# A planned transformer kernel: which matmuls the plan counts as a change, and where the next head's second projections stand

## The reference

```python
h = _attention(_rms(x, ln1_w[l]), wq[l], wk[l], wv[l], wo[l], cos, sin, causal_bias)  # 16 heads of 64, 4 key heads, causal
x = clip(res + h)
h = _moe(_rms(x, ln2_w[l]), wr[l], wg[l], wu[l], wd[l])     # router, softmax, top 2 of 8; all 8 experts computed, weighted
x = clip(res + h)
```

## Time and profile before

| | us |
|---|---|
| median of 3 runs | 3292.73 |
| profiled execution | 3282.75 |
| its span | 3280.9 |
| TensorE busy | 3071.8 (94%) |
| VectorE busy | 2605.9 (79%) |
| ScalarE busy | 2173.9 (66%) |
| GpSimd busy | 2014.9 (61%) |

### The profile page before, as it was taken

How to read it: one execution, slowest core, us unless ns; L and a number is a source line. 1 busy time by engine, 2 the same in 40 slices (tenths; PEclk the granted TensorE clock), 3 DMA queues, 4 the chain that set the end, 5 groups by cost and what they waited for, 6 DMA issues and landing times. The chain is left out here.

```text
span 3280.9 us, 50730 instructions
## 1 busy us (share of the span) xinstructions
PE 3071.8 (94%) x16864; PEld 2036.3 (62%) x16864; DVE 2605.9 (79%) x3764; ACT 2173.9 (66%) x4011; POOL 2014.9 (61%) x1573
## 2 busy tenths in 40 slices
PE   5999999799999999999999999999999999999998
PEld 3555555456666577666665776666657766666576
DVE  7788876678888678888886778888867888888677
ACT  4566667676666676766666767666667676666675
POOL 2100000377878676778776757787767677877675
PEclk8899999889999999999999999999999999999999
DMA  5442421323323065323230653233206532332053
GB/s 122 74 77 49 82 61 38 81 71 80 72 68 75 18 196 146 88 63 77 68 73 20 196 142 90 65 75 71 65 24 191 150 89 65 76 71 65 24 185 113
DMA packets 160402, 283.55 MB, mean 86 GB/s; under 512 B 32593, under 2 KB 64209, under 8 KB 159889
## 3 DMA queue, kind: packets, MB, share of 16 engines
q1 hardware_dynamic: 159632, 280.18, 33.9%
q10 hardware_dynamic: 512, 0.13, 0.0%
HBM read 88.47 MB, written 31.72 MB: 37 GB/s over the span
## 5 line engine op out<-in xcount | busy, mean ns | idle before, releaser
L1471 ACT ACTIVATE prob<-psA 128x512 f32<-128x512 f32 x1152 | 658.3, 593 | 510.7 <-PE psA L1869 328.4
L1273 POOL TENSOR_TENSOR xw<-xw,prob 128x512 f32<-128x512 f32 x672 | 872.4, 1298 | 169.3 <-ACT prob L1471 102.3
L2193 DVE TENSOR_REDUCE mxp<-psA 128x1 f32<-128x512 f32 (+3 forms) x864 | 527.6, 663 | 60.2 <-PE psA L1838 59.5
L2167 DVE RECIPROCAL rden<-psA 128x256 f32<-128x256 f32 x256 | 448.5, 1752 | 150.9 <-PE psA L1897 148.4
L1868 PE MATMUL psA<-qs,ks 128*128 128x512 f32 x1152 | 504.4, 438 | 14.3 <-ACT prob L1471 7.9
L1838 PE MATMUL psA<-ks,qs 128*128 128x512 f32 (+3 forms) x1536 | 438.4, 368 | 41.3 <-DVE ks L2295 16.8
L1273 POOL TENSOR_TENSOR xw<-prob 128x512 f32<-128x512 f32 x224 | 288.1, 1286 | 275.4 <-issue 169.9
L1869 PE MATMUL psA<-qs,ks 128*128 128x512 f32 x1152 | 454.1, 394 | 0.0
L1307 POOL TENSOR_TENSOR hidl<-gate,hidh 128x512 fp32r<-128x512 f32 x256 | 335.6, 1322 | 175.0 <-ACT hidh L1549 172.8
L1483 ACT ACTIVATE psA<-maskq 128x512 f32<-128x512 bf16 (+1 forms) x672 | 359.5, 556 | 82.5 <-DVE mxp L2193 55.5
L2115 DVE TENSOR_REDUCE mxp<-psA 128x1 f32<-128x1024 f32 x256 | 304.8, 1220 | 82.8 <-PE psA L1669 81.7
(11 more groups left out here) (222 smaller groups left out, 5855.6 us busy)
## 6 DMA issues: line engine op xcount, KB each, us to landing
qs<-normed SPq DMA_DIRECT2D x256, 256.0 KB, 4.2
rbp<-rab SPq DMA_DIRECT2D x256, 192.0 KB, 3.4
spread<-routing_weights SPq DMA_DIRECT2D x128, 256.0 KB, 3.6
qs<-qs SPq DMA_DIRECT2D x64, 256.0 KB, 3.9
expert_weight_halves<-eh SPq DMA_DIRECT2D x32, 384.0 KB, 3.7
expert_weight_halves<-el SPq DMA_DIRECT2D x32, 384.0 KB, 4.5
eh<-expert_weight_halves SPq DMA_DIRECT2D x32, 384.0 KB, 3.4
el<-expert_weight_halves SPq DMA_DIRECT2D x32, 384.0 KB, 4.1
```

The lines of the kernel that those rows point to most:

```text
L1273: g.tensor_tensor(psum_k[:, t % 2, :], before, prob[:, i % 4, :], ALU.add).then_inc(s_su, 1 if kt > 1 else 2 + (t == 1))
L1471: act(prob[:, k % 4, :], psS[:, k % 2, :], ACT.Exp, scale=float(HD) ** -0.5).then_inc(s_ex, 1)
L2167: vec.reciprocal(rden[:, :], psO[t % 2][:, 256:512]).then_inc(s_rd, 1)
L2193: vec.tensor_reduce(dst, bank, AX.X, ALU.max).then_inc(s_mr, 1)
```

## The change

Three things are changed.

- In MAIN the second projections of the next head, P(head+1, 1, u), move ahead of the last GQ = 4 shares of this head (the diagonal shares of t = 7) and its second J. Before, they stood behind that J.
- SEEDED is worked out with a record of what each bank was last filled with: a diagonal share is seeded if the last item in its bank that was not itself seeded was a P, a W or a share of the full 512 columns. Before, it was seeded if the item just before it in its bank existed and was not a J.
- The planner's `narrow` becomes "VDOJ" and its `switch` 105.

```diff
 for head in range(1, HEADS):
-    for half in range(NCH):
-        MAIN += chunk_maxima(head, half) + [("J", head, half)]
-        if (head, half) == (1, 0):
-            MAIN += [("W", j) for j in range(TPB // 2, TPB)]
-        MAIN += projections(head + 1, half) if head + 1 < HEADS else []
+    early, later = chunk_maxima(head, 0), chunk_maxima(head, 1)
+    ahead = [projections(head + 1, c) if head + 1 < HEADS else [] for c in range(NCH)]
+    MAIN += early + [("J", head, 0)]
+    if head == 1:
+        MAIN += [("W", j) for j in range(TPB // 2, TPB)]
+    MAIN += ahead[0] + later[:-GQ] + ahead[1] + later[-GQ:] + [("J", head, 1)]
...
-SEEDED = {item: None for item in EARLY + MAIN if item[0] == "M" and diagonal(*item[2:]) and BEFORE[item] and BEFORE[item][0] != "J"}
-SEEDED = {item: i for i, item in enumerate(SEEDED)}
+def width(t, m):
+    _, w, k0, k1 = max_pieces(t)[m]
+    return w * (k1 - k0)
...
+SEEDED, filled = {}, {}
+for item in EARLY + MAIN:
+    bank, share = BANK[item], item[0] == "M"
+    if share and diagonal(*item[2:]) and filled.get(bank):
+        SEEDED[item] = len(SEEDED)
+    else:
+        filled[bank] = item[0] in "PW" or share and width(*item[2:]) == CH
...
-    return planned(plan, kinds, 150, 150, "VD", 110, {"vector": 120})
+    return planned(plan, kinds, 150, 150, "VDOJ", 105, {"vector": 120})
```

## The result

| | before | after |
|---|---|---|
| median of 11 runs each | 3293.19 us | 3300.89 us |
| lowest, highest | 3286.01, 3296.85 | 3294.77, 3304.58 |
| profiled execution, its span | 3282.75, 3280.9 | 3303.45, 3301.6 |

The ratio of after to before is 1.0023 [1.0015, 1.0031], slower by 0.23%. That lies inside the predicted range (3274 to 3316), 5 us above its number, and just inside the part called slower (above 3299.3), which had a chance of 0.34. The profiled executions lie 20.7 us apart and the medians 7.7: the one of before was faster than all 11 of these runs, the one of after slower than its median. Lines after the change are 11 higher: V is L1893, D L1908, O L1915, M L1849, S L1879 and L1880, J L1859.

What follows compares the result with a forecast made beforehand. TensorE, busy 94% of the span, was taken as the bound. Terms 4.3 + 1 - 1 - 0.7 made +3.6 us on the profiled 3282.75, so 3286 profiled and 3296 for the median, range 3274 to 3316.

Steps and rivals of the forecast that it cites:

- -1.7: Second projections and masks together: put at -1 and -0.7 us.
- The blocks: Planner's new set on TensorE: 12 O go inside runs of V and D and break them, +4.3 us.
- Blocks stay 456 to 475: Main forecast's sign: O and J go to edges of V/D runs on TensorE; 3296 us, chance 0.38.
- B: Rival, slower: the set pulls V to O, cutting V/D runs into 40 more; 3311 us, chance 0.30.
- C: Rival, faster: held-back O lets S run, V/D runs grow to 3.4 and number 414; 3282 us, chance 0.32.
- 73 breaks: Upper end for the new set: every third of 220 attached O and J inside a V/D run, +26 us.
- Lone O: Sign on TensorE: O alone between S fall from about 138 to under 60, without time falling with it.
- The price of a block: On TensorE each run of V or D costs 0.36 us however long, plus 0.43 us for each V or D.
- The charge from 110 to 105: Planner's switch charge: moves a V/D run's price in the plan by 10 ns; put at 0.
- The delayed O: Later O delays VectorE's add into inner and the V behind it: +1 us, +7 if the wait doubles.
- Second projections: P moved ahead of the last four diagonal shares: nothing waits for them, -1 us, ends -11 and +3.
- Masks: Seeded shares per layer fall 168 to 162; 24 wide mask matmuls go, 48 narrow come: -0.7 us, ends -3 and +5.

Runs made afterwards that it cites:

- experiment 3: Kernel before with set VD and the planner's charge at 0: 3453.77 us, 1.049 of before.
- experiment 6: Changed kernel with each O or J between V and D on TensorE moved behind the V or D that follows: 3276.53 us, 0.9944 of before.
- experiment 7: Changed kernel with each layer's first J uncounted and O and J moved behind the blocks they break: 3258.75 us, 0.9888 of before.
- experiment 5: Changed kernel with only the first J of each layer's head 0 left out of the counted set: 3275.07 us, 0.9935 of before.
- experiment 4: Changed kernel with set VD and charge 180: 3281.81 us, 0.9964 of before.
- experiment 8: Changed kernel with set VD and charge 140: 3293.26 us, 1.0007 of before.
- experiment 1: Changed kernel's order of items and masks, with before's set VD and charge 110: 3265.16 us, 0.9919 of before.
- experiment 2: Kernel before with only the set VDOJ and charge 105: 3279.55 us, 0.9963 of before.
- experiment 10: Changed kernel with set VDO (no J counted), charge 105, and O moved behind the blocks: 3264.73 us, 0.9912 of before.

## Why the prediction was right, and where it was not

*The number* is right (3296 against 3300.9, inside the range, with nearly even chances for faster, the same and slower), but as a sum of terms that were wrong in both directions: -27 where -1.7 stood, and a loss of 26 from one J per layer that stood nowhere. That they all but cancelled is luck.

*The blocks.* "Blocks stay 456 to 475" failed narrowly (480). The sign is B's; B's mechanism is not what happened. No V was cut off because an O pulled it; O and J went inside existing blocks, 99 of them where I had 12. Free of charge in the plan, an O that stands ahead of V in the list is taken whenever it is ready during a block. I had asked where O is ready in the order of before, in which it had been placed at once; once O is held back, its place is wherever the next block is, and that includes its middle. That 99 breaks are only 24 more blocks is C's half of the story: the stretches of V, D, O and J without another matmul between them fell from 453 to 381 and hold 3.7 V or D each instead of 3.1, so the held-back O did gather V. Lone O fell from 138 to 37 and the time did not fall with it, as forecast. The upper end I gave for this step (73 breaks) was exceeded too.

*The price of a block.* 0.36 us holds for one block among full matmuls (0.33 here, 0.36 for the 428 single ones of experiment 3), 0.30 for the mean of many in the spacing (experiments 3, 6 and 7 against 5), and 0.27 in measured time. +24 blocks are +7 us of the 13 in the spacing; the other 6 come with the second edit, whose spacing is 8 above before with 4 blocks fewer. The rule of the Trainium skill ("TensorEngine Tiling (Array Packing)", Key Properties), that changing the tiling mode drains the engine, agrees with all of these; it gives no size. By it alone the wrong set is the one with O and J in it, and experiment 6, which only takes them out of the blocks, gains 24 us.

*The charge from 110 to 105.* Put at 0; not tried by itself. Higher charges (experiments 4 and 8) on the new list, with the set VD, showed that the plan's answer is not smooth: 180 is better than 140, and both are worse than 110.

*The delayed O.* Put at +1, doubled wait at +7. The wait on inner fell (7.3 to 4.1); the wait of O on att rose by 9.8. It stays at 16.6 with O moved behind (experiment 6) and 15.4 in 5 and 7, and is 0.4 with the second edit alone. It is not the set VDOJ that makes it, since the new list with VD and a charge of 140 or 180 has it too (22.5 and 36.1). In all of these it is first of all the O of tile 0, which in layer 1 stands right behind the last share of t = 7 and right ahead of the V of tile 1. Why VectorE is late with its input there is open.

*Second projections.* This is the term that was mis-sized: -1, with ends of -11 and +3, against -27 for it and the masks together (experiment 1). The prediction's own test said it: the wait behind ks stays near 17 us if the edit is worth nothing, "and under 8 if I am wrong there". It went to none; but it did so in experiment 2 as well, which has before's list, so that sign could not tell the edit from any new order, and how much of the -27 is the projections' own place is not shown. Two errors: I looked at the wait that the edit names and not at the other inputs that came just too late (att, inner and xw of VectorE and GpSimd, together 19.4 us before); and I took "TensorE has other work" as cover, though TensorE takes its list in order, and in each of these waits it stood idle.

*Masks.* The counts are right (x648, x56 of which 48 are narrow). Their worth is inside experiment 1 and was not tried alone. Waits behind mask copies rose, 13.1 to 18.4 us, and not the other way.

*What was missing.* The held J at the layer's head and the clock that falls behind it, 26 us (experiment 5; 19 of the 20 us between its split and that of after are clock). The prediction weighed every O and J as if it stood in the steady part of a head. It named J's own cost, 0.12 us, and never asked what stands behind J in its bank.

*The sum that the runs give.* Against before, in measured time: second edit -27; set and charge -13 alone. Together they would be -40 if they added; they are +8. Of those 48 us, 26 are the first J (the layer's head is intact in both single kernels: J stands 3 and 9 places behind its share). The other 22 are read from the split and no run isolates them: the stalls, 257 us before, fall to 213 and 199 singly and only to 227 together, so much of what either saved cannot be saved again; against this the spacing, +8 and +41 singly, is only +13 together.

## What to carry to other kernels

A planner's class of "expensive neighbours" should hold the operations for which the timeline shows a price at both edges. A member that is free on the chip is not harmless, because it is both delayed to join the class and let into the middle of it: with the new list that cost 36 us (experiment 1 against after). With those two faults mended afterwards the larger class was no worse (experiments 7 and 10 against 1: -6 and 0 us), so the faults were what cost, not the counting. Look at each rare place where such an item stands alone (a layer's head, a ring of two banks): there a delay of 21 us shows on no line of the page and moves everything behind it. Two reorderings that may live off the same stalls must be timed together; -27 and -13 made +8 here, and a small repair of the finished order (experiment 7) then gave -1.1%.

## What the runs showed of the hardware

- With TensorE idle 0.2 to 1.1 us at a time at the layer's head the granted clock of the window was 0.72, and 0.63 in the one of experiment 8; the time at the 1.2 GHz level from the first layer on was 51 us before, 111 after, 77 in experiment 1. At that level the 512-column matmuls of S start 0.43 us apart (1323.90, 1324.33 in after) instead of 0.23: the matmuls that could have caught up the delay are slow too.
- A mask matmul of 128 columns took 0.23 us by the profile, the longest of the wider ones 0.39.
- The price of leaving and entering the 128*64 matmuls is about the same whether the matmuls outside are float32 (O) or rounded (S, M): 0.33 us for an O inside three V, 0.36 for a V or D between rounded ones.
